# Cross attentions: fp32 scores taken straight from the projections, two heads at a time in different quarters of PE's rows, and the softmax sums by a column of ones

## What is computed

```python
def cross(x, ctx, mask, Wq, bq, Wk, bk, Wv, bv, Wo, bo):     # x [16,112,256], ctx [16,375,256]
    q, k, v = heads(x @ Wq + bq), heads(ctx @ Wk + bk), heads(ctx @ Wv + bv)   # 16 heads x 16
    s = einsum('bhqd,bhkd->bhqk', q, k) / 4
    s = where(mask == 0, very_negative, s)
    a = softmax(s, axis=-1)                                  # [16 batches, 16 heads, 112, 375]
    y = einsum('bhqk,bhkd->bhqd', a, v)
    return merge(y) @ Wo + bo
x = layernorm(x + cross(...))
```

## Time and profile before

| | |
|---|---|
| median of three runs | 2536.01 us (2535.88 to 2540.05) |
| the profiled execution, its time | 2537.32 us |
| its span, first to last instruction | 2535.6 us |
| mean granted clock of PE | 0.948 of full speed |
| first cross attention, from the first score matmul to the last | 139.0 to 501.2 us |
| second one | 1269.3 to 1634.4 us |

### The profile page before, as it was taken

One profiled execution on the slowest core, in us unless ns is written; L12 is line 12 of the kernel. 1 busy time (PEld: TensorE's weight loads), 2 busy tenths in 40 slices (PEclk: granted clock), 3 DMA queues, 4 the chain that ended last, 5 costly groups with the idle time before them and its releaser, 6 DMA issues. The chain is left out here.

```text
span 2535.6 us, 47865 instructions
## 1 busy us (share of the span) xinstructions
PE 2269.8 (90%) x15451; PEld 1853.6 (73%) x15451; DVE 1701.2 (67%) x4282; ACT 1306.0 (52%) x3186; POOL 510.4 (20%) x399
## 2 busy tenths in 40 slices
PE   8789999859999977888699999889999999999995
PEld 5567777748999855555477777668888888888884
DVE  2466677755888755666467767677777867777665
ACT  3266666745666624444266667644444444444441
POOL 3200000011111142222200000003333333333333
PEclk9899999979999978889799999999999999999998
DMA  3065655323766411000165566222323233322222
GB/s 112 7 158 117 130 121 113 76 77 103 224 202 212 148 51 34 0 0 0 42 148 122 118 130 127 66 77 95 107 78 111 89 96 106 94 90 92 72 74 72
DMA packets 201754, 246.48 MB, mean 97 GB/s; under 512 B 58481, under 2 KB 176706, under 8 KB 201602
## 3 DMA queue, kind: packets, MB, share of 16 engines
q1 hardware_dynamic: 198050, 235.37, 35.4%
q0 software_dynamic: 3552, 9.18, 1.2%
HBM read 202.95 MB, written 41.55 MB: 96 GB/s over the span
## 5 line engine op out<-in xcount | busy, mean ns | idle before, releaser
L827 ACT ACTIVATE cross_pr<-cross_sc,cross_mn 112x375 f32<-112x375 f32 x512 | 310.4, 606 | 232.4 <-DVE cross_mn L917 231.5
L917 DVE CUSTOM_DVE_ANT_0 cross_sc<-cross_ps,cross_masked 112x375 f32<-112x375 f32 x512 | 273.0, 543 | 177.4 <-PE cross_ps L715 156.1
L2327 POOL TENSOR_TENSOR switch_gl<-switch_gb,switch_gh 128x896 fp32r<-128x896 f32 x128 | 270.8, 2116 | 574.4 <-ACT switch_gh L2508 574.4
L723 PE MATMUL cross_ps<-all_ident,cross_pr 112*125 112x112 f32 x1536 | 256.6, 276 | 23.6 <-DVE cross_pt L924 22.3
L2564 DVE SCALAR_TENSOR_TENSOR switch_vt<-switch_ps,switch_chosen,switch_vt 112x128 f32<-112x128 f32 x512 | 144.1, 344 | 191.5 <-PE switch_ps L106 186.9
L723 PEld LDWEIGHTS cross_ps<-all_ident,cross_pr 112*125 112x125 f32 x1536 | 234.7, 190 | 44.1 <-DVE cross_pt L924 26.6
L715 PE MATMUL cross_ps<-cross_k,cross_q 96*112 96x376 f32 x512 | 223.0, 436 | 15.3 <-DMA cross_k<-cross_k_dram 10.9
L104 PE MATMUL switch_ps<-switch_vw,switchgates_xh 128*112 128x512 f32 x512 | 209.0, 408 | 4.9 <-ACT switch_vt L2487 4.9
L104 PE MATMUL switch_ps<-switch_gh,switch_ow 128*128 128x448 f32 x512 | 192.4, 376 | 18.5 <-POOL switch_gl L2327 17.2
L106 PE MATMUL switch_ps<-switch_vw,switchgates_xl 128*112 128x512 f32 x512 | 202.4, 395 | 0.0
L105 PE MATMUL switch_ps<-switch_vw,switchgates_xh 128*112 128x512 f32 x512 | 201.7, 394 | 0.0
(11 more groups left out here) (386 smaller groups left out, 5561.0 us busy)
## 6 DMA issues: line engine op xcount, KB each, us to landing
switch_gb<-switch_gt_rows SPq DMA_DIRECT2D x128, 448.0 KB, 3.6
experts_w_raw<-in_L_ffn_w_dram SPq DMA_DIRECT2D x42, 1024.0 KB, 5.5
cross_k<-cross_k_dram SPq DMA_DIRECT2D x96, 375.0 KB, 8.2
cross_k_dram<-cross_ks SPq DMA_DIRECT2D x32, 750.0 KB, 4.6
all_place<-in_ctx_dram SPq DMA_DIRECT2D x32, 375.0 KB
cross_q<-cross_q_dram SPq DMA_DIRECT2D x192, 56.0 KB, 4.4
all_place<-in_L_ffn_v_w_dram SPq DMA_DIRECT2D x16, 512.0 KB, 6.2
all_place<-in_L_ffn_o_w_dram SPq DMA_DIRECT2D x8, 1024.0 KB, 7.3
```

Of the source, the lines that this page charges most:

```text
L723: last = nc.tensor.transpose(ps[0:KP, TURNED + h % 2, t * T:(t + 1) * T], pr[:, h % NB, t * KP:(t + 1) * KP], ident[0:T, 0:T])
L827: nc.scalar.activation(pr[:, h % NB, :], sc[:, h % NB, :], ACT.Exp, bias=mn[parity][:, h:h + 1], scale=-1.0, accum_out=rs[parity][:, h:h + ...
L917: nc.vector.tensor_tensor_reduce(out=sc[:, h % NB, :], in0=ps[0:T, SCORES + h % 2, 0:S2], in1=mask_of[:], scale=-0.25, scalar=3e38, op0=AL ...
L2327: pool.tensor_tensor(gl[u % 2][:], gb[u % RING][:], gh[u % 2][:].bitcast(F32), ALU.subtract)\
```

## The change

- Queries and keys stay in SBUF as they come out of the projections, in full fp32: `kt` (keys) and `q`, which holds every query twice, once for the even heads and once for the odd ones of each 32 rows, with the other head's rows multiplied by zero (`of_copy`, made by POOL and DVE before the loop; `q_bias` likewise). The DRAM tiles, `store`, `stack`, the low halves and two thirds of the stack are gone.
- A head's scores are an fp32 matmul over 32 rows (one quarter) and 375 columns. `scores` now runs at even steps only and issues two heads, in different quarters of the rows, into the two banks; it waits for both heads before them.
- Heads are taken in another order, `head(i)`, so that neighbours lie in different quarters; the output is put back in order by two multiplies in DVE's `tail` instead of one.
- The sums of the softmax no longer come from ACT's exponential (`accum_out`): `vv` gets a 17th column of ones, and DVE takes the reciprocal from PSUM after the output was turned.
- Projections are made one batch ahead for all units; before the loop for batch 0 only. `FRONT_AT` is re-dealt on all engines, and V2 is brought out by DVE at step 1 of its own batch.
- SP only loads the context and the mask.

```diff
-        ks = s.sb("ks", [P, 2 * DC, S2], F32R)
-        qs = s.sb("qs", [P, 2 * DC, T], F32R)
-        k_dram = [s.dram(f"k_dram{b}", [2 * D, S2]) for b in range(2)]
-        q_dram = [s.dram(f"q_dram{b}", [2 * D, T]) for b in range(2)]
-        kk = [s.sb(f"k{b}", [3 * PAIR, H // 2, KEYS], F32R) for b in range(2)]
-        q = [s.sb(f"q{b}", [3 * PAIR, H // 2, 2, T], F32R) for b in range(2)]
+        kt = [s.sb(f"k{b}", [P, DC, S2]) for b in range(2)]
+        q = [s.sb(f"q{b}", [P, DC, 2, T]) for b in range(2)]
+        of_head = s.sb("of_head", [P, P // HD])
+        of_copy = s.sb("of_copy", [P, 2])
+        q_bias = s.sb("q_bias", [P, DC, 2])
...
+        def head(i):
+
+            return i // 8 * 8 + i % 4 * 2 + i % 8 // 4
...
-            def scores(b, parity, h):
-                if h == 0:
-                    wait_front_read(pe, b, V2)
-                    pe.wait_ge(q_stacked, (b + 1) * Q_PARTS * 16)
-                    pe.wait_ge(k_stacked, (b + 1) * K_PARTS * 16)
-                wait(pe, s_max, b * H + h - 1)
-                nc.tensor.matmul(ps[0:T, SCORES + h % 2, 0:KEYS], q[parity][:, h // 2, h % 2, :],
-                                 kk[parity][:, h // 2, :], start=True, stop=True).then_inc(s_done, 1)
+            def scores(b, parity, i):
+
+                if i == 0:
+                    pe.wait_ge(f_act, act_count(b, K1))
+                wait(pe, s_max, b * H + i)
+                for h in (i, i + 1):
+                    quarter = slice(h % 4 * 32, h % 4 * 32 + 32)
+                    nc.tensor.matmul(ps[0:T, SCORES + h % 2, 0:S2], q[parity][quarter, h // 8, h % 8 // 4, :],
+                                     kt[parity][quarter, h // 8, :], start=True, stop=True).then_inc(s_done, 1)
...
-            FRONT_AT = {2: V0, 4: V1, 6: V2, 7: C0, 8: C1, 10: Q, 12: K0, 14: K1}
+            FRONT_AT = {1: C0, 3: C1, 5: Q, 7: K0, 9: K1, 11: V0, 13: V1, 15: V2}
...
                 for i in range(H):
-                    scores(b, parity, i)
+                    if i % 2 == 0:
+                        scores(b, parity, i)
...
-            for u in (C0, C1, Q, K0, K1):
-                front(-1, 0, u)
             for u in range(UNITS):
-                front(0, 0 if u in (V0, V1, V2) else 1, u)
+                front(0, 0, u)
...
+            act.wait_ge(copies_ready, 2)
...
                     for m in range(DC):
-                        last = nc.scalar.activation(qs[:, m, :], bank[:, m * T:(m + 1) * T], ACT.Identity,
-                                                    bias=qk_bias[:, 0, m:m + 1])
+                        for n in range(2):
+                            last = nc.scalar.activation(q[parity][:, m, n, :], bank[:, m * T:(m + 1) * T], ACT.Identity,
+                                                        bias=q_bias[:, m, n:n + 1], scale=of_copy[:, n:n + 1])
...
-                                     scale=-1.0, accum_out=rs[parity][:, h:h + 1]).then_inc(exped, 1)
+                                     scale=-1.0).then_inc(exped, 1)
...
-                    ch.link(nc.vector.reciprocal(ri[:], rs[parity][:]))
                     dve.wait_ge(t1_done, b + 1)
-                    nc.vector.tensor_tensor(otok[:], ps[0:T, TAIL, :].rearrange("p (h e) -> p h e", e=32)[:, :, 0:HD],
-                                            ri[:].unsqueeze(2).broadcast_to([T, H, HD]), ALU.mult).then_inc(otok_ready, 1)
+                    ch.link(nc.vector.reciprocal(ri[:], ps[0:T, TAIL, :].rearrange("p (h e) -> p h e", e=32)[:, :, HD]))
+                    turned = ps[0:T, TAIL, :].rearrange("p (a n e d) -> p n a e d", n=2, e=4, d=32)
+                    by = ri[:].rearrange("p (a n e) -> p n a e", n=2, e=4)
+                    ordered = otok[:].rearrange("p (a e n) d -> p n a e d", n=2, e=4)
+                    for n in range(2):
+                        last = nc.vector.tensor_tensor(ordered[:, n], turned[:, n, :, :, 0:HD],
+                                                       by[:, n].unsqueeze(3).broadcast_to([T, H // 8, 4, HD]), ALU.mult)
+                    last.then_inc(otok_ready, 1)
...
-            FRONT_AT = {5: V0, 6: V1, 7: V2, 11: Q, 13: K0, 15: K1}
+            FRONT_AT = {13: V0, 15: V1}
```

More of the change, by code:

```diff
@@ L514, in over_batches @@
             batch(B - 1, 1, "last")
[L516 to L520, removed]
+        def head(i):
+            return i // 8 * 8 + i % 4 * 2 + i % 8 // 4
         def done_count(g, u):
-            return g * UNITS + FIRST_UNITS + u + 1
+            return g * UNITS + u + 1
         def act_count(g, u):
-            return g * ACT_UNITS + ACT_UNITS + ACT_ORDER[u]
+            return g * ACT_UNITS + u + 1
         def dve_count(g, u):
-            return g * DVE_UNITS + FIRST_DVE + DVE_ORDER[u]
+            return g * DVE_UNITS + u - V0 + 1
         def wait_front_read(engine, g, u):
@@ L639, in _ @@
             pool.memset(half[:], -0.5).then_inc(const_ready, 1)
+            c = Chain(pool, pool_chain)
+            c.link(pool.memset(of_head[:], 1.0))
+            c.link(pool.affine_select(out=of_head[:], in_=of_head[:], compare_op=ALU.is_ge, fill=0.0, base=0,
+                                      pattern=[[-HD, P // HD]], channel_multiplier=1))
+            c.link(pool.affine_select(out=of_head[:], in_=of_head[:], compare_op=ALU.is_ge, fill=0.0, base=HD - 1,
+                                      pattern=[[HD, P // HD]], channel_multiplier=-1))
+            for b in range(2):
+                c.link(pool.memset(vv[b][:], 0.0))
+                last = pool.memset(vv[b][:, :, :, HD:HD + 1], 1.0)
+            last.then_inc(v_zero, 1)
             def convert_mask(b, parity):
@@ L774, in batch @@
                         turn(b - 1, i - TL + H)
-                    if FRONT_AT.get(i) in units:
-                        u = FRONT_AT[i]
-                        front(b + 1, 1 - parity if u in (V0, V1, V2) else parity, u)
+                    if i in FRONT_AT and not last:
+                        front(b + 1, 1 - parity, FRONT_AT[i])
                     if not first and i in TAIL_AT:
@@ L848, in _ @@
             TAIL_AT = {5: 0, 9: 1, 15: 2}
-            FRONT_AT = {7: C0, 8: C1, 10: Q, 12: K0, 14: K1}
+            FRONT_AT = {2: C0, 4: C1, 6: Q, 8: K0, 10: K1}
             def batch(b, parity, kind):
-                first, units = kind == "first", units_of(kind)
+                first, last = kind == "first", kind == "last"
                 for i in range(H):
@@ L861, in batch @@
                     exponent(b, parity, i)
-                    if FRONT_AT.get(i) in units:
-                        front(b + 1, FRONT_AT[i])
+                    if i in FRONT_AT and not last:
+                        front(b + 1, 1 - parity, FRONT_AT[i])
                     if not first and TAIL_AT.get(i, 0) > 0:
                         tail(b - 1, TAIL_AT[i])
-            for g in (-1, 0):
-                for u in (C0, C1, Q, K0, K1):
-                    front(g, u)
+            for u in (C0, C1, Q, K0, K1):
+                front(0, 0, u)
             over_batches(act, batch)
@@ L954, in batch @@
                     maximum(b, parity, i)
-                    if FRONT_AT.get(i) in units:
-                        u = FRONT_AT[i]
-                        front(b + 1, 1 - parity if u in (V0, V1, V2) else parity, u)
+                    if i == 1:
+                        front(b, parity, V2)
+                    if i in FRONT_AT and not last:
+                        front(b + 1, 1 - parity, FRONT_AT[i])
                     if not first and i in TAIL_AT:
```

151 lines of the change are left out of this document (40 added, 111 removed).

## The result

The changed kernel takes 2575.18 us (median of 4 runs, 2570.74 to 2575.75) against 2535.95 for the kernel before; the ratio is 1.0155, with a 95% interval of 1.0128 to 1.0181. It is 39 us slower where I had forecast 91 us slower. The direction holds and the time lies in the 8-in-10 range (2550 to 2715), but it lies outside the forecast's own range (2590 to 2675), and the change is less than half as large as forecast.

A forecast was written before the change was run, and what follows sets the result against it. PE was taken to bound the kernel: middle batches grow 3.6 us to 27.2, 120.8 us over two stages, less 25 + 5 at stage starts, +91 on 2536 gives 2627 us; own range 2590 to 2675, 8-in-10 range 2550 to 2715.

The forecast's parts named there:

- the change of shape: On PE, going to a quarter of the rows and back: late starts and bare weight loads, 0.40 us a pair.
- the period of a middle batch: Cross-attention loop: 26.2 us of PE work plus 1.0 of waits, 27.2 us, 3.6 more than before.
- The pair at 1.13 us: Two heads' scores on PE: 0.63 streaming, 0.40 shape change, 0 to 0.2 weight loads; the old pair cost 0.36.
- The waits at 1.0 us a batch: PE's waits in a middle batch of cross attention: 1.0 us in all, down from 3.6.
- half as many hand-overs: Cross-attention loop: issuing scores in pairs leaves half the hand-overs, one reason for waits of 1.0 instead of 3.6 us.
- the low halves: Queries and keys on DVE (0.61 us for each key half): waits for them vanish, second reason for the smaller waits.
- The clock came back: First batch of each attention: without the pause before it, the granted clock of 0.86 recovers, 2.6 us a stage.
- waits stay: Rival, cross-attention loop: waits remain 3.6 us a batch instead of 1.0, 80 us more, 2707 us; chance 0.14.
- by halves: Rival, score pairs on PE: in-order starts make a pair take three records, 79 us more, 2706 us; chance 0.08.
- not at all: Rival, score pairs on PE: the two quarters don't run side by side, 161 us more, 2788 us; chance 0.05.
- Half hidden: Rival, score pairs: weight loads slip under the run-out, a pair costs 0.90, waits 0.5, 2553 us; chance 0.16.
- Faster: Rival, score pairs: shape change costs next to nothing, a pair of 0.63 gives 2499 us; chance 0.10.

The follow-up runs named there:

- same_quarter: Changed kernel with the two heads of a pair in the same quarter of the rows, so they run one after the other: 2752.8 us, ratio 1.0858.
- full_rows: Changed kernel with each score matmul over all 128 rows instead of 32 (scores not the reference's, for time alone): 2632.4 us, ratio 1.0376.
- b_ahead: Kernel before with each head's scores issued singly but one step earlier, as many hand-overs as before: 2475.0 us, ratio 0.9777.
- a_late: Changed kernel with each pair of scores issued one step later, at the head of the odd step: 2629.3 us, ratio 1.0364.
- b_thin: Kernel before with DVE's low halves of queries and keys cut to two columns each, losing precision: 2513.0 us, ratio 0.9916.
- b_pairs: Kernel before with the scores of two heads issued together at even steps, still fp32r over 96 rows: 2467.2 us, ratio 0.9747.
- accum: Changed kernel with softmax sums taken again by ACT's exponential (accum_out) and the reciprocal from there; the column of ones stays unread: 2570.2 us, ratio 1.0146.
- values_first: Changed kernel with `values` issued right behind the pair of scores, ahead of the turn, in steps 0, 4, 8 and 12: 2553.4 us, ratio 1.0060.

## Why the prediction was right and wrong

The bound was read rightly: PE was the fuller engine, and matmul time added to a pair shows in the total (178 us in `same_quarter`, where 0.62 x 256 is 159, and 57 in `full_rows`, where 0.26 x 256 is 67).

What a pair does was right too: two quarters side by side, 0.63 us, and about 0.4 us for the change of shape. The step that failed is the period of a middle batch, put at 27.2 us; it is 25.5. Two of its terms were too large, the second one for a wrong reason.

- *The pair at 1.13 us.* I added 0.1 for the second head's weight loads, which "queue behind the first's". They don't: PE lists the four records of a pair within 0.89 us in all, and the next turn starts at 0.82. The pair costs 1.0 us, 0.13 x 256 = 33 us less. L1706, one matmul without a partner, could not show this; L736, whose neighbours' loads do overlap, could have, and I did not use it for the loads. The value 1.03, without any queueing, was the lower end of my range for this price.
- *The waits at 1.0 us a batch.* PE now stands 0.3 us a batch, and its forecast work with pairs of 1.0 us is 17.1 + 8.0 = 25.1 of 25.5 us: 0.7 x 31 = 22 us less. Of the two reasons that I gave, half as many hand-overs was wrong as the main one: `b_ahead` gets most of the gain of pairs from the lead alone, and `a_late` shows waits coming back with the hand-overs still halved. The other, the low halves, holds for the smaller part (`b_thin`, 0.9 us a batch). Had I asked which of PE's waits start with late scores on DVE, the lead of every second head would have stood out. Pairs took 2 us a batch from the kernel before, so that the change, measured against `b_pairs` with the same order of issue, loses 3.9 us a batch (25.5 against 21.6), half paid for by an order of issue that has nothing to do with fp32 or quarters. By PE's work alone it would be (1.00 - 0.36) x 8 = 5.1; what the new `FRONT_AT` and the missing low halves give of the difference was not tried.

Together these are 55 us too much, which alone would bring 91 to 36, next to the 39 measured. That it comes so close is partly luck, because the other terms were off as well and cancel. Both attentions together, in us, after less before, from PE's starts in the two profiles:

| stretch | forecast | measured |
|---|---|---|
| from PE's first instruction to the first scores | -25 | -28.7 |
| the two first batches, clock included | 7.2 - 5 = +2 | +11.2 |
| the 26 middle batches | +93.6 | +49.2 |
| the two last but one | +12.8 | +8.8 |
| the two last, to the end of their output | +7.2 | +0.9 |
| all that lies between and behind | 0 | -3.8 |
| sum | +91 | +37.6 |

The clock came back in one attention only. In the first one 0.81 was granted in the first batch, lower than the 0.86 of before, and the batch took 26.6 us; in the second one it was 1.00 where it had been 0.87, and the batch took 21.9 us. That is 4.7 us between two batches of the same shape. In the first attention the clock stood at 0.50 (1.2 GHz) from 132 to 140 us, after PE had stood 0.9 of the 6 us from 126 to 132; in the second one it was already at 0.50 when PE began, behind idle stretches of 2.5 and 1.5 us, and back at 1.00 from 1275 us, before the first scores. But even at 1.00 the batch is 3.3 us longer than before, where the corrected terms, 1.9 for pairs and waits less 2.6 for the clock, would make it 0.7 shorter; why is not shown. Nor is it shown why the last batches hardly grew.

My range has a slip too: a pair of 1.03 to 1.24 and waits of 0.5 to 1.8 give 2586 to 2680, not 2590 to 2675.

Of the rivals, "waits stay", "by halves" and "not at all" are refuted by the runs. "Half hidden" was nearest in total, at 2553, and wrong in detail: the weight loads of the change of shape stay bare (a pair costs 1.0, not 0.90), and waits of 0.3 are left, not 0.5. "Faster" asked for a pair under 0.78 us; it is 1.0. Two row tiles in fp32 run side by side here with nothing lost (0.62 us saved of 0.63). The Trainium skill's 3.07 of 4 (TensorE: Matmul & The Clock Gate, Part 3) is for four tiles, which no run here had.

That sums by a column of ones are free on PE is confirmed by `accum`; that SP's DMAs inside the loop were worth nothing was not tested by itself.

## What to carry to other kernels

Ask of an in-order engine not how often it waits but what it issues just before a long block: work that another engine needs next belongs ahead of that block. Moving the scores up by one head was worth 2.2% of this kernel's time, with not one instruction fewer, though PE's own idle time hardly changed.

Narrow matmuls in quarters of the rows pay only in company: two side by side save a full matmul, but entering and leaving costs 0.37 us, so put everything that uses quarters next to each other (22 us here), and compare with the fp32r way before giving it up.

When a change bundles several edits, put each into the old kernel alone: the good one here was hidden behind a larger loss.

## What the runs showed of the hardware that was not expected

Two matmuls in different quarters of the rows start their first records together, weight loads included: in the pair at 305.58 us the trace's single records start 6 ns apart (305.581 and 305.587), then 0.40 us later again 6 ns apart, and the weight loads 7 ns apart. The four records span 0.89 us, where two heads in one quarter span 1.51.

The same entry into a quarter costs the same for one matmul or two side by side: behind the last full matmul the pair starts 0.09 us late, its first records take 0.40 us instead of 0.315, the next turn comes 0.40 us behind the second ones, and the turn after that 0.09 us late. In `same_quarter` the steps from record to record are 0.41, 0.32, 0.31 and 0.40, so only the first and the last are long.

A change between two quartered shapes, rows to columns, costs no more than a change between a quartered one and the full array: in `values_first` 0.82 us pass from the pair's start to the start of `values` (300.17 to 300.99), as they do to the turn in the change (305.58 to 306.40).
